# Attention block on one Trainium2 core: parts stored in two transfers per tile pair, stacks loaded in runs of terms between projection tiles

## The reference

```python
x = x + attention(_layernorm(x))         # x: (2, 1024, 512) float32
x = x + ffn(_layernorm(x))
# attention: qkv = clip(x @ Wqkv.T, -8, 8); q, k get a layer norm with weights;
#   32 heads of 16; scores = q k^T * 16**-0.5 + slope_h * (j - i), causal; softmax; @ v; @ Wout.T
# ffn: x @ W_q.T with W_q = sum over 4 of alphas[k] * bases[k]   (bases are +1/-1)
```

## Time and profile before

| | us |
|---|---|
| median of three runs (lowest to highest) | 751.18 (749.0 to 751.19) |
| profiled execution, device time | 752.16 |
| its span, first to last instruction | 750.4 |

### The profile page before, as it was taken

One profiled execution on the slowest core, in us unless ns is written; L12 is line 12 of the kernel. 1 busy time (PEld: TensorE's weight loads), 2 busy tenths in 40 slices (PEclk: granted clock), 3 DMA queues, 4 the chain that ended last, 5 costly groups with the idle time before them and its releaser, 6 DMA issues.

```text
span 750.4 us, 16038 instructions
## 1 busy us (share of the span) xinstructions
PE 684.3 (91%) x6096; PEld 410.7 (55%) x6096; DVE 573.3 (76%) x990; ACT 414.2 (55%) x855; POOL 312.3 (42%) x403
## 2 busy tenths in 40 slices
PE   3999999993929799999999999999999999399998
PEld 3888888871305344544444444444445442378886
DVE  6798899974929699999899979899899830176654
ACT  4133332231007788888788868788788888222221
POOL 1477677773111362542642633113222323544440
PEclk9999999995558899999999999999999999699999
DMA  8225555564676234334433442343434201444441
GB/s 286 85 76 160 154 158 169 154 182 136 190 200 184 96 104 127 106 97 118 126 96 100 119 129 74 108 132 86 122 102 120 73 23 37 124 138 138 136 150 72
DMA packets 102828, 93.64 MB, mean 125 GB/s; under 512 B 12408, under 2 KB 82680, under 8 KB 102752
## 3 DMA queue, kind: packets, MB, share of 16 engines
q1 hardware_dynamic: 100640, 90.52, 41.8%
q0 software_dynamic: 2112, 2.10, 1.2%
HBM read 57.44 MB, written 33.82 MB: 122 GB/s over the span
## 4 chain that ended last, share of the span: by engine, by line
PE 61%; SPq 16%; DMA 8%; DVE 6%; issue 5%; POOL 2%; ACT 2%; DVEq 0%; POOLq 0%; ACTq 0%
PE ps L1068 19%; PE ps L1103 18%; SPq L400 9%; PE ps L1049 7%; PE ps L983 5%; PE ps L985 4%; PE ps L984 4%; SPq L433 4%; DMA second_q<-shift_lo 2%; DMA x_in<-in_x 2%; PE ps L1045 2%; SPq L484 1%; PE ps L991 1%; DVE qk_stat L867 1%; DMA wout_raw<-in_wout_t 1%
## 5 line engine op out<-in xcount | busy, mean ns | idle before, releaser
L922 DVE TENSOR_REDUCE stats<-ps 128x1 f32<-128x512 f32 (+3 forms) x608 | 362.1, 656 | 68.2 <-PE ps L1049 65.0
L752 ACT ACTIVATE probs<-ps 128x512 f32<-128x512 f32 (+2 forms) x640 | 312.8, 558 | 94.4 <-PE ps L1068 88.9
L1049 PE MATMUL ps<-first_k,first_q 54*128 54x128 bf16 (+3 forms) x1152 | 225.7, 285 | 13.8 <-issue 10.9
L1068 PE MATMUL ps<-first_q,first_k 54*128 54x512 bf16 (+3 forms) x768 | 197.2, 332 | 22.5 <-DMA second_q<-shift_lo 18.1
L1068 PE MATMUL ps<-second_q,second_k 64*128 64x128 bf16 (+4 forms) x1152 | 203.2, 276 | 0.0
L1103 PE MATMUL ps<-probs,v_sb 128*32 128x512 f32 (+3 forms) x1536 | 165.0, 502 | 1.6 <-issue 0.7
L649 POOL TENSOR_SCALAR_AFFINE_SELECT probs<-probs 128x256 f32<-128x256 f32 x256 | 102.4, 406 | 143.0 <-ACT probs L752 137.6
L1068 PEld LDWEIGHTS ps<-first_q,first_k 54*128 54x128 bf16 x768 | 56.7, 95 | 149.1 <-ACT probs L752 118.9
L1049 PEld LDWEIGHTS ps<-first_k,first_q 54*128 54x128 bf16 x1152 | 93.9, 96 | 53.8 <-DVE stats L922 26.5
L1068 PEld LDWEIGHTS ps<-second_q,second_k 50*128 50x128 bf16 (+1 forms) x1152 | 92.8, 96 | 21.8 <-issue 2.6
L983 PE MATMUL ps<-wqkv_hi,xt_hi 128*128 128x512 f32 x192 | 77.3, 403 | 0.0
(11 more groups left out here) (79 smaller groups left out, 783.7 us busy)
## 6 DMA issues: line engine op xcount, KB each, us to landing
parts_dram<-parts SPq DMA_DIRECT2D x96, 128.0 KB, 2.2
v_dram<-v_ext SPq DMA_DIRECT2D x16, 512.0 KB, 3.4
v_sb<-v_dram SPq DMA_DIRECT2D x16, 512.0 KB, 4.2
o_dram<-o_sb SPq DMA_DIRECT2D x32, 256.0 KB
first_q<-parts_dram SPq DMA_DIRECT2D x96, 64.0 KB
first_k<-parts_dram SPq DMA_DIRECT2D x96, 64.0 KB
second_q<-parts_dram SPq DMA_DIRECT2D x96, 64.0 KB
second_k<-parts_dram SPq DMA_DIRECT2D x96, 64.0 KB
```

What stands on the lines that cost most here:

```text
L752: act.activation(weights, scores, ACT.Exp, scale=SCALE).then_inc(exp_done, 1)
L922: dve.tensor_reduce(to, scores, AX.X, ALU.max).then_inc(max_taken, 1)
L1049: last = pe.matmul(ps[:, bank, r * cols:(r + 1) * cols], first_q[n % STACKS][rows, hp, i * P:(i + 1) * P], first_k[n % STACKS][rows, hp, k ...
L1068: return pe.matmul(ps[:, bank, r * cols + first:r * cols + last], stack_k[n % STACKS][rows, heads[r] // PAIR, kb * P:(kb + 1) * P], stack_ ...
```

## The change

The scratch tensor for the parts gets a new layout: for each head row six slots (three of q, three of k), and within a slot both halves and both head pairs. One slot of a row for one half is 4 KB without a gap. A pair of tiles is stored in two transfers instead of twelve, one for q and one for k. The stack tiles are filled by runs: neighbouring terms whose slots are neighbours come in one transfer of 32 or 48 rows. With the terms reordered, each first tile takes two transfers per half (16 and 32 rows), each second tile one (48 rows), so that a stack takes 12 term transfers and 6 of bias rows. First and second tiles have semaphores of their own, and PE waits for the first ones before the maxima and for the second ones before the scores. Stacks 0 and 1 are loaded in tile steps 10 to 13, a quarter in each. After the last tiles SP loads v of groups 0 and 1, then writes the shift rows of group 0, then stores the last parts, then loads the last weights, and only then stack 2. POOL loads `bases` in step 14 of group 0, once `alphas` has arrived.

```diff
-TERMS = [(0, 0), (0, 1), (1, 0), (1, 1), (0, 2), (2, 0)]
+TERMS = [(0, 0), (0, 1), (1, 0), (0, 2), (1, 1), (2, 0)]
+SLOTS = [slice(0, 6, 5), slice(1, 5, 3), slice(2, 4, 1)]
+def term_runs(i, terms):
+    at = [term[i] if i == 0 else 5 - term[i] for term in terms]
+    runs = []
+    for r, slot in enumerate(at):
+        if runs and slot == at[r - 1] + 1:
+            runs[-1][1].append(slot)
+        else:
+            runs.append((r, [slot]))
+    return [(r, slots[0], len(slots)) for r, slots in runs]
-STACKS_AT = 14
+STACKS_AT = 10
-    parts_dram = nc.dram_tensor("parts_dram", [2, 3, PAIR, BATCH, GPB * HD, PAIR, SEQ], BF16).ap()
+    parts_dram = nc.dram_tensor("parts_dram", [BATCH, GPB * HD, 6, PAIR, PAIR, SEQ], BF16).ap()
...
-                    for n in range(3):
-                        for i in range(2):
-                            for half in range(PAIR):
-                                sp.dma_start(
-                                    parts_dram[i, n, half, tt // TPB, :, :, ds((tt % TPB) * P, 2 * P)],
...
+                    for i in range(2):
+                        sp.dma_start(parts_dram[tt // TPB, :, 3 * i:3 * i + 3, :, :, ds((tt % TPB) * P, 2 * P)]
+                                     .rearrange("r s e a t -> r (s e a) t"),
...
+            def load_terms(n, i, dst, terms, loaded):
+                for half in range(PAIR):
+                    for r, slot, many in term_runs(i, terms):
+                        at = half * HALF_ROWS + r * HD
+                        sp.dma_start(dst[at:at + many * HD, :, :].rearrange("p a t -> p (a t)"),
+                                     parts_dram[n // GPB, n % GPB * HD:(n % GPB + 1) * HD, slot:slot + many, half]
+                                     .rearrange("d s a t -> s d (a t)")).then_inc(loaded, 16)
...
+                    load_first(0)
+                if s == STACKS_AT + 1:
+                    load_second(0)
+                if s == STACKS_AT + 2:
+                    load_first(1)
+                if s == STACKS_AT + 3:
+                    load_second(1)
...
+            run_tiles(sp, tile_step_and_stacks, -1, TILES)
+            sp.wait_ge(v_done, TILES)
+            for n in range(2):
+                load_values(n)
+            load_shift(0)
+            run_tiles(sp, tile_step, TILES + 1, TILES + 1)
             projections_over()
+            load_last_weights()
...
-                pool.wait_ge(v_loaded[0], 16)
+                pool.wait_ge(alphas_loaded, 4 * 16)
...
-                if s == -EARLY:
+                if s == BASES_AT:
                     load_bases()
...
-                    pe.wait_ge(stack_loaded[n % STACKS], 16 * (4 + STACK_LOADS * (n // STACKS + 1)))
+                    pe.wait_ge(first_loaded[n % STACKS], 16 * FIRST_LOADS * (n // STACKS + 1))
...
+                    pe.wait_ge(second_loaded[n % STACKS], 16 * (STEP_LOADS + SECOND_LOADS * (n // STACKS + 1)))
```

More of the change, by code:

```diff
@@ L42 @@
 PAIR = 2
+BY_HALF = [c % PAIR * PAIR + c // PAIR for c in range(DC)]
 HALF_ROWS = P // PAIR
@@ L155 @@
 EARLY_STEPS = 8
-STACKS_AT = 14
-assert STACKS_AT - 2 >= TPB and STACKS_AT % 4 == 2
-STACK_LOADS = 2 * PAIR * 2 * NT + 2 * PAIR + PAIR
+STACKS_AT = 10
+assert STACKS_AT - 2 == TPB
+FIRST_LOADS = PAIR * sum(len(term_runs(i, TERMS[:NT])) + 1 for i in range(2))
+SECOND_LOADS = PAIR * sum(len(term_runs(i, TERMS[NT:])) for i in range(2)) + PAIR
+STEP_LOADS = 2 * PAIR
+BASES_AT = 14
 WFFN_AT = [NE + NE // 3 + 2 * NE * c for c in range(DC)]
@@ L303, in build @@
         parts_stored = [sem(f"parts_stored{i}") for i in range(2)]
-        stack_loaded = [sem(f"stack_loaded{i}") for i in range(STACKS)]
+        first_loaded = [sem(f"first_loaded{i}") for i in range(STACKS)]
+        second_loaded = [sem(f"second_loaded{i}") for i in range(STACKS)]
         v_loaded = [sem(f"v_loaded{i}") for i in range(2)]
@@ L357, in run_groups @@
         def run_groups(eng, step):
-            run(eng, step, -2, GROUPS)
+            run(eng, step, 0, GROUPS)
         def run_outputs(eng, step):
@@ new lines, in load_bias, with load_first @@
+            def load_bias(n, i, dst, row, last, loaded):
+                for half in range(PAIR):
+                    at = half * HALF_ROWS + NT * HD
+                    sp.dma_start(dst[at:at + last - row, :, :], bias_rows[i, n % GPB, half, row:last]).then_inc(loaded, 16)
+            def load_first(n):
+                for i, dst in ((0, first_q[n % STACKS]), (1, first_k[n % STACKS])):
+                    load_terms(n, i, dst, TERMS[:NT], first_loaded[n % STACKS])
+                    load_bias(n, i, dst, 0, BIAS_ROWS, first_loaded[n % STACKS])
@@ L424, in load_stack, with load_second @@
+            def load_second(n):
+                loaded = second_loaded[n % STACKS]
+                for i, dst in ((0, second_q[n % STACKS]), (1, second_k[n % STACKS])):
+                    if n < STACKS:
                         for half in range(PAIR):
                             at = half * HALF_ROWS + SECOND_K
[L426 to L441, removed]
@@ L478, in group_step @@
                 n = s + 1
[L479 to L486, removed]
+                if 1 <= n < GROUPS:
+                    load_shift(n)
                 if s == GROUPS - 2:
@@ L580, in tile_step @@
                     pair = parts[t // 2 % 2]
-                    pool.tensor_tensor(pair[:, 2, :, :, half], rest[:], pair[:, 1, :, :, half],
+                    pool.tensor_tensor(pair[:, SLOTS[2], :, half], rest[:], pair[:, SLOTS[1], :, half],
                                        ALU.subtract).then_inc(lo_ready, 1)
@@ L703, in tile_step @@
                     if t >= 4 and t % 2 == 0:
-                        act.wait_ge(parts_stored[t // 2 % 2], 12 * 16 * (t // 4))
-                    act.activation(parts[t // 2 % 2][:, 0, :, :, half],
+                        act.wait_ge(parts_stored[t // 2 % 2], 2 * 16 * (t // 4))
+                    act.activation(parts[t // 2 % 2][:, SLOTS[0], :, half],
                                    ps[:, QKT_BANK:QKT_BANK + 2, :].rearrange("p i (c t) -> p i c t", c=DC),
@@ L716, in tile_step @@
                     act.wait_ge(rest_ready, t + 1)
-                    act.activation(parts[t // 2 % 2][:, 1, :, :, half], rest[:], ACT.Copy).then_inc(mid_ready, 1)
+                    act.activation(parts[t // 2 % 2][:, SLOTS[1], :, half], rest[:], ACT.Copy).then_inc(mid_ready, 1)
                 t = s
@@ L986, in product, with turn @@
                 return last
-            def turn(bank, rows):
-                for c in range(DC):
-                    last = pe.transpose(ps[:, bank, c * P:(c + 1) * P], rows[:, c * P:(c + 1) * P], ident[:])
+            def turn(bank, rows, places=range(DC)):
+                for c, place in enumerate(places):
+                    last = pe.transpose(ps[:, bank, place * P:(place + 1) * P], rows[:, c * P:(c + 1) * P], ident[:])
                 return last
```

55 lines of the change are left out of this document (28 added, 27 removed).

## The result

| | before | after |
|---|---|---|
| median of four runs each (lowest to highest), us | 750.09 (747.63 to 751.19) | 827.91 (825.34 to 828.95) |
| span of the profiled execution, us | 750.4 | 827.2 |
| mean granted clock of the span | 0.945 | 0.903 |

The changed kernel is slower by 10%: ratio 1.103, 95% interval 1.1004 to 1.1056. The forecast was 833 with 780 to 930.

The account below looks back on a forecast made before the run. PE bound projection and groups before. Forecast: group 0 starts at 217, group 1 at 263, groups 1 to 13 at 31.3 us (407) end at 670, the rest 161.8: span 832, median 833 us, range 780 to 930.

Parts of the forecast that it names:

- Which engines a run uses: Stack loads: a run of two or three terms uses two or three DMA engines, always the lowest, instead of sixteen.
- The price of a packet: Stack loads: 167 ns per queued 4 KB packet, 23.0 us for 138 on the lowest engine; other bound 253 ns, 34.9.
- A group: Groups 1 to 13: lowest engine needs 31.3 us (stack 23.0, sums' stores 6.2, v 1.9, ending packets 0.2) against PE's 25.1.
- Half clock: Groups 1 to 13: a slower clock after each wait is hidden in the 6 us that PE waits.
- Projection: End of projection: x of tile 15 lands at 158 instead of being used at 143.47, 14.5 us uncovered.
- Group 0: From its start T, queued parts, weights, stack 2, `bases` and stores take until T + 46.2; group 1 starts at 263.
- (1): Projection to group 0: stack 0 is there when projection ends, so the maxima come 9.7 us sooner.
- (2): From the join of the maxima to group 0: 7.1 to 7.5 us instead of 20.9, gain 13.8.
- (4): Groups 1 to 13: average could fall from 25.6 to 25.1 us, 6.5 us, if shorter loads stop delaying shift rows.
- (3): Group 0: weights asked for before they are needed, so it could lose its excess of 6.2 us.
- the rival of sixteen engines: Stack loads: runs spread over sixteen engines after all, so only the gains stand, 716 us; chance 0.05.
- What I said the profile would show: Profile after: groups about 31 us, PE waiting some 6 before each, shift rows landing far above 3.1, DMA share 0.2 to 0.3.

Follow-up runs that it names:

- the third experiment: Changed kernel with runs of three kept in the second tiles, first tiles loaded term by term: 794.56 us, ratio 1.059 to the kernel before.
- the second experiment: Changed kernel with the same 12 term transfers per stack, each read with 16 head rows outermost: 727.77 us, ratio 0.9698 to the kernel before.
- the last experiment: Changed kernel, rows outermost, sums' stores cut in 4, `bases` later, output weights before stack 2's first tiles, `alphas` after group 1's shift rows: 717.05 us.

## Why the prediction was right, step by step

**Which engines a run uses.** Right, and shown in three ways: 2.9 engines busy, 6328 packets, and 100 us for the order of one index. The rule that the Trainium skill gives in "DMA: Bandwidth & Descriptors", section "Why a DMA increments its semaphore by 16 and not by 1", holds here to the packet for the number of engines. Which engines they are, no row names.

**The price of a packet.** I took 167 ns, the weight load's. The 174 of the stretch shown is too high, since besides 69 packets of 4 KB it holds 64 of 512 B. A stretch in which the runs of three are read and nearly nothing else:

```profile
426.50:430.00 3.50, 3.39 (x47) 1.98 (x43) 2.74 (x6) 3.07 (x8) 1.75 (x5) 1.00 0.19 77
```

77/(0.19 x 16) = 25.3 GB/s for an engine, 162 ns. That my price came so near is partly luck. The weight load went in packets of 2 KB, and I divided its 393 GB/s by 16 engines, not by its share of 1.05 x 16, as I did for the single packets; that would have given 23.4 GB/s and 175 ns.

**A group.** Predicted 31.3 us, measured 30.7 on average, between 28.5 and 33.1. In the changed kernel the mechanism was right too. I said that the lowest engine never rests, and by the trace's packets fewer than one DMA engine is busy in only 7 of the 799 half microseconds of groups 1 to 13. With 162 ns the sum is 138 x 0.162 + 8.3 = 30.7. The 8.3 was never measured in this kernel, so that it fits to the tenth is chance. But as a general rule the sum is too simple. It takes the lowest engine's total as the period, and that failed in the third experiment: 22.0 by the sum, 28.7 measured, with all DMA engines at rest before the load of a long group. There the period is a chain from the start of the load to the landing of the shift rows. In the changed kernel that chain is: the shift rows made 18.3 to 20.7 us into a group (from its first exponentials on ACT to `shift_lo` on POOL), their issue, and a landing of 5 to 6.7 us. In some groups SP is held up too:

```profile
307.43 10.59 SPq L517 DMA_DIRECT2D o_dram<-o_sb  x2
318.07 3.09 SPq L488 DMA_DIRECT2D second_q<-shift_hi  x2
```

The shift rows of that group were made by 314.9 and issued from 318.07 on. When all of a stack is confined, engine and chain come to about the same; when half of it is, only the chain tells.

**Half clock.** I held it hidden in the wait, and most of it is. PE's waits before four groups (that before group 8, 3.25 us at 481.73, stands above), and the six microseconds after each (granted clock third from the end):

```profile
295.54 0.37 PE L1104 MATMUL ps<-first_q,first_k 54*128 54x512 bf16 x1 [1.40 <-issue]
...
296.00:302.00 6.00, 6.00 (x75) 2.46 (x71) 5.70 (x10) 5.08 (x11) 1.75 (x5) 1.00 0.29 79
...
328.23 0.58 PE L1104 MATMUL ps<-first_q,first_k 54*128 54x512 bf16 x1 [7.45 <-issue]
...
329.00:335.00 6.00, 6.00 (x52) 1.95 (x50) 3.62 (x6) 3.03 (x6) 0.81 (x2) 0.60 0.19 70
...
482.00:488.00 6.00, 6.00 (x48) 1.93 (x44) 3.19 (x5) 2.48 (x5) 0.81 (x2) 0.55 0.25 81
...
604.17 0.37 PE L1104 MATMUL ps<-first_q,first_k 54*128 54x512 bf16 x1 [2.12 <-issue]
...
605.00:611.00 6.00, 6.00 (x81) 2.58 (x82) 5.46 (x10) 5.19 (x11) 2.03 (x5) 1.00 0.28 82
```

After 1.40 and 2.12 us PE kept 2.4 GHz (1.00) and the next shift rows were made 18.3 us into the group, as in nearly every group of the kernel before. After 7.45 and 3.25 us it was mostly at 1.2 GHz, and they came at 20.4 and 20.5. In 6 us at half clock PE gets through 48 to 52 matmuls rather than 75. So the rows are made 2 us later, but it isn't shown that the next group starts later by it. The two groups at full clock, 2 and 12, took 33.1 and 32.7 us, longer than any other. And where a free engine lands a row in 1.7 us, the last one took 5.0 to 6.7 here, so rows issued 2 us sooner would, as I read it, have stood behind the same work. What the clock changed is how PE spends the group: 27.3 us busy (354.81/13) and 3.4 idle, where it had 25.3 busy before and I had forecast 6 idle.

**Projection.** Predicted that x of tile 15 is 14.5 us late. The two x that DVE waited for, and the join of the maxima:

```profile
137.74 0.69 DVE L868 BATCH_NORM_STATS2 x_stat<-x_in 128x6 f32<-128x512 f32 x1 [5.71 <-DMA x_in<-in_x]
...
157.20 0.69 DVE L868 BATCH_NORM_STATS2 x_stat<-x_in 128x6 f32<-128x512 f32 x1 [11.51 <-DMA x_in<-in_x]
...
208.12 0.25 DVE L927 TENSOR_REDUCE peak<-stats 128x32 f32<-128x96 f32 x1
```

Tile 15 is used 157.20 - 143.47 = 13.7 us later than before. The join comes 208.12 - 203.60 = 4.5 us later, which is some 14 late less the 9.7 expected from the earlier stack. From the join to group 0 it took 6.1 us (predicted 7.1 to 7.5, 20.9 before), and group 0 started at 214.24 instead of the predicted 217.

**Group 0.** Predicted 46 us, measured 51.9. The term that was too small is the first one, `alphas` and weights at 393 GB/s until T + 11.5, with T the start of group 0. Their landing, and what all transfers together moved before `bases` was asked for:

```profile
L433 SPq DMA_DIRECT2D wout_raw<-in_wout_t x1: 437/437/437, 221.5 to 221.5; - x1
...
DMA to landing us min/median/max: 10.3/10.3/10.3
...
219.60:227.90 8.30, 8.30 (x115) 4.52 (x115) 7.62 (x14) 6.61 (x15) 1.99 (x6) 1.00 0.74 233
```

The weights landed at 231.8, T + 17.5, so 6.0 us later than I had it. From there to the start of group 1 it took 34.3 us, where my terms add up to 34.7. Why they moved 233 GB/s and not 393 stays open. PE stood still for much of this, and of its wait for the first tiles of stack 2 I had only said that they come late:

```profile
247.96 0.60 PE L1084 MATMUL ps<-first_k,first_q 54*128 54x512 bf16 x1 [16.10 <-DMA first_k<-in_bias_rows]
...
266.12 0.58 PE L1104 MATMUL ps<-first_q,first_k 54*128 54x512 bf16 x1 [6.71 <-issue]
```

PE stood for 16.1 us in the middle of the group, so the maxima of group 1 and its shift rows were late as well, and the last of these needed 12.2 us to land. Against the prediction group 0 is 6 us longer, groups 1 to 13 are 8 shorter together, and group 0 starts 3 earlier: the 5 us between the predicted span of 832 and 827.2.

**The gains.** (1) and (2) came, all but 1.4 of the 23.5 us: with the runs spread, group 0 starts at 202.4. (4), 0.5 us per group, came in the second experiment. (3), group 0's excess of 6.2 us, did not: ACT no longer waits for the weights, but PE waits for stack 2, which now stands behind the parts, `alphas` and the weights. So the rival of sixteen engines, priced at 716, would in truth have given 727.8; the missing 12 us are 9.5 in group 0, 1.4 before it and 0.9 after the start of group 14. Only the last experiment, with group 0 at 25.0, reached 717.

**What I said the profile would show.** Wrong in one place: PE waits 3.6 us before a group on average (50.9/14), not some 6. In another it only looks wrong: the median landing of the shift rows did not rise (2.8 us, 3.1 before), and one row of each pair seems to land in 2.3 to 3.2 us. But the four rows of a group count on one semaphore, 16 increments each, and the profile takes every 16th as the landing of the next row. For group 8 the trace has 48 of the 64 increments by 477.24, which it gives to the first three rows, and the last four at 481.09 to 481.64, 0.2 us apart. They look like one late engine's shares of all four rows, so that all four were late; no row names the engine. Only the landing of the last row of a group can be read from such a view, and that is what PE waits for.

## What to carry to other kernels

Before merging transfers, write down the outermost count of both sides: three terms outermost put a 192 KB load on three DMA engines, the same ones each time, and the same load with 16 rows outermost used all. Ask next what small transfer is issued behind it and who waits for that, and add up the chain from the start of the load to that landing; the total work of the busy engine is only a lower bound. And where a merge saves issues, check whether the data's landing was hidden behind them.

## What the runs showed of the hardware that I had not expected

- The issue itself is held up behind confined transfers. SP's store of sums took 0.57 us to issue before (median; highest 0.64), 1.03 after with a highest of 10.56, and 0.58 again with rows outermost. That the queues of the lowest engines were full is my reading; no row shows a queue's depth. A landing time counted from the issue doesn't hold this delay.
- 4 KB packets that queue on an engine took 162 ns, against 253 ns for single ones.
- Confinement isn't priced by its number of packets: 82 per group cost more (28.7 us) than 86 (26.8). That it is because they started later is argued, not shown.
